# A layer of attention and routed experts: rows and activations of the routed stage turned by VectorE and ScalarE instead of TensorE

## The reference

```python
x = x + cross_attention(layernorm(x), ctx_1024)        # 1024 tokens of 512, 1601 keys each of 16 batches
x = x + relative_attention(layernorm(x), ...)
x = x + ffn(layernorm(x), ...)                         # ffn is a block of its own:
#   x = x + mla(rmsnorm(x, w_ln1), ...)
#   x = x + moe(rmsnorm(x, w_ln2), ...)
def moe(xn, ...):                                      # xt: 1024 tokens x 512
    shared = silu(xt @ Wg_s) * (xt @ Wu_s) @ Wd_s
    probs = sigmoid(xt @ W_router + routing_bias)      # 7 experts
    scores, idx = top_k(probs, 2)
    scores = scores / sum(scores)
    for each of the two experts e of a token:          # Wg_r, Wu_r, Wd_r are 7 x 512 x 512
        out += score * ((silu(xt @ Wg_r[e]) * (xt @ Wu_r[e])) @ Wd_r[e])
    return shared + out
```

## Time and profile before

| | us |
|---|---|
| median of 3 runs | 813.64 |
| lowest and highest | 810.62, 814.64 |
| profiled execution, whole | 809.95 |
| profiled execution, its span | 808.1 |
| mean granted TensorE clock | 0.994 of full speed |

### The profile page before, as it was taken

The page is one execution under the profiler, slowest core; times in us unless marked ns, Lnnn a source line. Parts: engine busy times, 40 slices in busy tenths (PEclk is TensorE's granted clock), DMA queues, the critical chain, the costliest instruction groups (busy, mean ns, idle before and its releaser), DMA issues.

```text
span 808.1 us, 17427 instructions
## 1 busy us (share of the span) xinstructions
PE 773.6 (96%) x6752; PEld 574.0 (71%) x6753; DVE 517.4 (64%) x1125; ACT 355.5 (44%) x913; POOL 301.0 (37%) x157
## 2 busy tenths in 40 slices
PE   4799999999899999989999999899999999999996
PEld 3555455554657778878867877788888888888884
DVE  5799798788652447777788887855364333443335
ACT  4356545661443248852178768523432122211221
POOL 1000000000442833732032213533649999993034
PEclk9999999999899999999999999999999999999999
DMA  9968756683520050040388000030485355531138
GB/s 341 390 252 327 259 218 243 262 326 122 219 105 1 0 149 13 2 138 0 105 312 314 1 0 1 22 137 25 183 306 210 112 206 167 191 135 52 52 114 275
DMA packets 46576, 127.04 MB, mean 157 GB/s; under 512 B 4001, under 2 KB 8353, under 8 KB 40369
## 3 DMA queue, kind: packets, MB, share of 16 engines
q1 hardware_dynamic: 36752, 105.44, 35.9%
q10 hardware_dynamic: 7200, 12.32, 4.4%
q0 software_dynamic: 2560, 8.39, 3.1%
HBM read 101.99 MB, written 24.15 MB: 156 GB/s over the span
## 4 chain that ended last, share of the span: by engine, by line
PE 81%; DVE 5%; DMA 5%; POOL 3%; ACT 3%; issue 2%; SPq 0%; DVEq 0%; ACTq 0%; POOLq 0%
PE scores L611 11%; PE bank L641 11%; PE bank L1137 7%; PE bank L1139 7%; PE bank L1138 7%; DMA nat<-in_ctx_keys 3%; PE bank L691 2%; POOL picked L1379 2%; PE bank L845 2%; PE bank L693 2%; PE bank L851 2%; PE bank L692 2%; PE bank L846 2%; PE bank L626 2%; PE bank L881 2%
## 5 line engine op out<-in xcount | busy, mean ns | idle before, releaser
L1844 DVE STREAM_TRANSPOSE ctxT<-nat 128x1024 f32<-128x1024 f32 (+3 forms) x124 | 116.9, 1004 | 7.8 <-DMA nat<-in_ctx_keys 7.5
L641 PE MATMUL bank<-nat,probT 128*64 128x512 f32 (+1 forms) x416 | 93.9, 597 | 0.1
L1366 POOL TENSOR_TENSOR ring_lo<-ring_raw,ring_hi 128x2048 fp32r<-128x2048 f32 x18 | 83.0, 4611 | 14.5 <-ACT ring_hi L1732 13.3
L1244 POOL TENSOR_TENSOR wq_lo<-wq_raw,wq_hi 128x1024 fp32r<-128x1024 f32 x4 | 9.3, 2352 | 207.6 <-ACT wq_hi L1477 207.6
L1137 PE MATMUL bank<-ring_hi,xg_lo 128*128 x180 | 74.2, 412 | 0.0
L1139 PE MATMUL bank<-ring_hi,xg_hi 128*128 x180 | 70.6, 392 | 0.0
L1138 PE MATMUL bank<-ring_lo,xg_hi 128*128 x180 | 70.1, 389 | 0.0
L2488 DVE TENSOR_TENSOR rhm_lo<-bank,rhm_hi 128x512 fp32r<-128x512 f32 x21 | 14.5, 692 | 80.2 <-ACT rhm_hi L1743 80.2
L641 PEld LDWEIGHTS bank<-nat,probT 128*64 128x64 f32 (+1 forms) x416 | 27.9, 136 | 51.6 <-issue 48.1
L1749 ACT COPY hn<-bank 128x512 f32<-128x512 f32 x22 | 12.9, 588 | 112.0 <-PE bank L1139 112.0
L611 PE MATMUL scores<-ctxT,hn 32*64 32x416 f32 (+8 forms) x1536 | 55.2, 426 | 5.1 <-issue 2.7
(11 more groups left out here) (317 smaller groups left out, 1936.1 us busy)
## 6 DMA issues: line engine op xcount, KB each, us to landing
nat<-in_ctx_keys SPq DMA_DIRECT2D x48, 1024.0 KB, 8.1
ring_raw<-in_Wexp SPq DMA_DIRECT2D x21, 1024.0 KB, 6.3
x_slots<-zeros SPq DMA_DIRECT2D x1, 5632.0 KB, 18.2
y_slots<-zeros SPq DMA_DIRECT2D x1, 5632.0 KB, 32.7
hn<-x_slots ACTq DMA_DIRECT2D x22, 256.0 KB, 4.5
y_slots<-hn ACTq DMA_DIRECT2D x22, 256.0 KB, 3.0
w_raw<-in_Wexp SPq DMA_DIRECT2D x3, 1024.0 KB, 5.3
nat<-in_ctx_keys SPq DMA_DIRECT2D x16, 130.0 KB
```

The lines of the kernel that those rows point to most:

```text
L641: last = nc.tensor.matmul(context_bank(k)[64 * b:64 * b + 64, :], probT[0:n, j, 64 * b:64 * b + 64], nat[k % 2][0:n, b, j, :], start=j == ...
L1366: last = nc.gpsimd.tensor_tensor(ring_lo[at], ring_raw[at], ring_hi.bitcast(F32)[at], ALU.subtract)
L1844: dve.transpose(dst, src).then_inc(columns_ready, 1)
```

## The change

Four things are changed.

1. **Rows.** `xg` is loaded by four DMAs of 32 partitions each instead of one of 128. Each moves 128 pieces of 512 bytes (`slot_rows`), and they are issued three tiles ahead. DVE turns the tile in blocks of 32 x 32 straight into PSUM (`xgT`, banks 6 and 7). The order of the features that comes out is made good by weights that are permuted before the launch (`by_block`). The low part's last quarter waits for the expert's weights (`rows_end`).
2. **Activations.** After its multiplication DVE turns `rhm` in 32 x 32 blocks into `rhm_blocks`. ACT moves these by 16 copies of 32 partitions x 128 elements to their places in bank 3. DVE makes both the high and the low part. The last tile keeps PE's transposes. On DVE the rows of tile t+2 are prepared between the multiplication and the split of tile t. On ACT the 16 copies of tile t come before the output of tile t-1.
3. **Entrance.** The second expert's down matrix is loaded as soon as the shared expert's products are done, and the other two when the first two tiles' rows have landed. POOL and ACT take the down matrix first (`order_of`, `second_high(2)`). DVE prepares the rows of tile 0 before it adds the output of block 6 and before the low part of the first expert's down matrix.
4. **Router.** Each of its matmuls becomes four of 32 columns of weights.

```diff
-        xg = hn[0:2]
+        xg = [t.rearrange("p (g f) -> p g f", f=P) for t in hn[0:2]]
+        xgT = [b[:].rearrange("p (a q) -> p a q", q=P) for b in bank[6:8]]
+        rhm_blocks = place(156, "rhm_blocks", [P, HC, 4, B32])
+        rhmT = bank[3][:].rearrange("p (c q) -> p c q", q=P)
+        def slot_rows(t):
+            return x_slots[ds(t * P, P), :].rearrange("(g q) (c f) -> c q g f", q=B32, f=P)
+        def order_of(e):
+            return (2, 0, 1) if e == 1 else (0, 1, 2)
...
                     sp.wait_ge(gu_full, NJ)
-                    sp.wait_ge(scattered, 16 * 2 * NT)
-                for m in range(3):
+                for m in order_of(e):
+                    if e == 1 and m == 0:
+                        for landed in xg_loaded:
+                            sp.wait_ge(landed, 64)
...
                 for c in range(HC):
-                    last = nc.tensor.matmul(bank[3][:, NE * k:NE * k + NR], xf[k % 4][:, c, :], wrout_sb[:, c, :],
-                                            start=c == 0, stop=c == HC - 1)
+                    for m in range(P // B32):
+                        own = slice(B32 * m, B32 * (m + 1))
+                        last = nc.tensor.matmul(bank[3][own, NE * k:NE * k + NR], xf[k % 4][:, c, own], wrout_sb[:, c, :],
+                                                start=c == 0, stop=c == HC - 1, skip_group_check=True)
...
             def load_rows(t, par):
-                nc.scalar.dma_start(xg[par][:], x_slots[ds(t * P, P), :]).then_inc(xg_loaded[par], 16)
+                for c in range(HC):
+                    nc.scalar.dma_start(xg[par][B32 * c:B32 * (c + 1)], slot_rows(t)[c]).then_inc(xg_loaded[par], 16)
             def hidden_columns_out(t):
-                act.wait_ge(rhmT_full, t + 1)
-                nc.scalar.copy(hidden_parts(t)[0][:].rearrange("p c q -> p (c q)"), bank[3][:]).then_inc(rhm_split, 1)
+                act.wait_ge(rhm_turned, 2 * t + 1)
+                if isinstance(t, int) and t == TILES - 1:
+                    last = nc.scalar.copy(rhm_last[0][:].rearrange("p c q -> p (c q)"), bank[3][:])
+                else:
+                    for g in range(4):
+                        for a in range(4):
+                            last = nc.scalar.copy(rhmT[B32 * a:B32 * (a + 1), :, B32 * g:B32 * (g + 1)],
+                                                  rhm_blocks[B32 * g:B32 * (g + 1), :, a, :])
+                last.then_inc(rhm_split, 1)
+            act.wait_ge(slots_ready, 5)
+            second_high(2)
             act.wait_ge(scattered, 16 * 2 * NT)
...
             def routed_step(t, par, turn, load=True):
                 if load:
-                    act.wait_ge(xgT_full, t + 1)
-                    load_rows(t + 2, par)
+                    act.wait_ge(xgT_full, t + 2)
+                    load_rows(t + 3, 1 - par)
                 routed_silu(t)
-                if isinstance(t, int) and t == TILES - 1:
-                    hidden_columns_out(t)
-                    output_rows(t - 1, 1 - par, turn)
-                else:
-                    output_rows(t - 1, 1 - par, turn)
-                    hidden_columns_out(t)
+                hidden_columns_out(t)
+                output_rows(t - 1, 1 - par, turn)
...
+            def rows_columns(t, par, turn):
+                dve.wait_ge(xg_loaded[par], 64 * turn)
+                dve.transpose(xgT[par].rearrange("p a (g q) -> p a g q", q=B32),
+                              xg[par].rearrange("p g (a e) -> p a g e", e=B32)).then_inc(xgT_full, 1)
...
             def routed_mult(t):
                 dve.tensor_tensor(rhm[:], rhm[:], bank[2][:], ALU.mult).then_inc(rhm_ready, 1)
+                if not (isinstance(t, int) and t == TILES - 1):
+                    dve.wait_ge(rhm_ready, t + 1)
+                    dve.transpose(rhm_blocks[:].rearrange("p c a q -> p (c a q)"), rhm[:]).then_inc(rhm_turned, 1)
             def hidden_split(t):
+                dve.tensor_copy(rhm_hi[:], rhmT).then_inc(rhm_turned, 1)
+                dve.wait_ge(rhm_turned, 2 * t + 2)
+                dve.tensor_tensor(rhm_lo[:], rhmT, rhm_hi.bitcast(F32)[:], ALU.subtract).then_inc(rhmT_ready, 1)
...
+            def hidden_and_next(t, par, turn):
+                nth = need_of(t + 2)
+                routed_mult(t)
+                rows_columns(t + 2, par, turn + 1)
+                hidden_split(t)
+                rows_end(par, nth)
```

More of the change, by code:

```diff
@@ L1140, in routed_product, with routed_hidden @@
                 last.then_inc(full, 1)
-            def rows_columns(t, par, turn):
-                pe.wait_ge(xg_loaded[par], 16 * turn)
-                if not (isinstance(t, int) and t < 2):
-                    pe.wait_ge(xgT_ready, t - 1)
-                for c in range(HC):
-                    last = nc.tensor.transpose(bank[6 + par][:, c * P:(c + 1) * P], xg[par][:, c * P:(c + 1) * P], ident)
-                last.then_inc(xgT_full, 1)
-            def routed_hidden(t, par, at, turn=None):
-                if not (isinstance(t, int) and t < 2):
-                    hidden_columns(t - 1)
+            def routed_hidden(t, par, at):
                 pe.wait_ge(xgT_ready, t + 1)
@@ L1223, in _ @@
             routed_hidden(TILES - 1, 1, at[1])
-            hidden_columns(TILES - 1)
+            last_hidden_columns()
             routed_output(TILES - 2, 0, at[0])
@@ L1359, in _ @@
             for e in range(1, NR):
-                for m in range(3):
+                for n, m in enumerate(order_of(e)):
                     pool.wait_ge(routed_loaded[m], 16 * (e + 1))
@@ L2452, in down_out @@
                 dve.tensor_tensor(y[:, k, :], bank[k % 4][:], y[:, k, :], ALU.add).then_inc(down_added, 1)
-            for k in range(NT - 1):
-                down_out(k)
-                if 3 <= k < 6:
-                    m = k - 3
-                    dve.wait_ge(split_hi, m + 1)
-                    at = (slice(None), PLACES[0], m)
-                    last = dve.tensor_tensor(ring_lo[at], ring_raw[at], ring_hi.bitcast(F32)[at], ALU.subtract)
-                    if m == 2:
-                        last.then_inc(split_ready, 1)
@@ L2467, in rows_columns_out @@
                 dve.wait_ge(xgT_full, t + 1)
-                columns = [bank[6 + par][:, c * P:(c + 1) * P] for c in range(HC)]
-                weights = [vec[:, V_W2 + c:V_W2 + c + 1] for c in range(HC)]
                 for c in range(HC):
-                    last = dve.tensor_scalar(xg_hi[par][:, c, :], columns[c], weights[c], None, ALU.mult)
+                    last = dve.tensor_scalar(xg_hi[par][:, c, :], xgT[par][:, c, :], vec[:, V_W2B + c:V_W2B + c + 1], None, ALU.mult)
                 last.then_inc(xg_split, 1)
@@ L2473, in rows_columns_out, with rows_low @@
                 dve.wait_ge(xg_split, t + 1)
-                dve.wait_ge(split_ready, nth)
-                for c in range(HC):
-                    last = dve.scalar_tensor_tensor(xg_lo[par][:, c, :], columns[c], weights[c], xg_hi[par].bitcast(F32)[:, c, :],
-                                                    ALU.mult, ALU.subtract)
-                last.then_inc(xgT_ready, 1)
+                for c in range(HC - 1):
+                    rows_low(par, c)
+            def rows_low(par, c):
+                return dve.scalar_tensor_tensor(xg_lo[par][:, c, :], xgT[par][:, c, :], vec[:, V_W2B + c:V_W2B + c + 1],
+                                                xg_hi[par].bitcast(F32)[:, c, :], ALU.mult, ALU.subtract)
@@ L2480, in routed_mult, with rows_end @@
+            def rows_end(par, nth=None):
+                if nth is not None:
+                    dve.wait_ge(split_ready, nth)
+                rows_low(par, HC - 1).then_inc(xgT_ready, 1)
             def routed_mult(t):
@@ L2491, in _ @@
-            rows_columns_out(0, 0)
-            down_out(NT - 1)
-            rows_columns_out(1, 1)
-            routed_mult(0)
-            hidden_split(0)
-            with dve.Fori(0, TILES // 2 - 1) as i:
+                if isinstance(t, int) and t == TILES - 1:
+                    hi, lo = rhm_last
+                    dve.tensor_tensor(lo[:].rearrange("p c q -> p (c q)"), bank[3][:],
+                                      hi.bitcast(F32)[:].rearrange("p c q -> p (c q)"), ALU.subtract).then_inc(rhmT_ready, 1)
+                    return
@@ new lines, in hidden_split @@
+                if not (isinstance(t, int) and t == 0):
+                    dve.wait_ge(rdown_full, t)
+                dve.tensor_copy(rhm_hi[:], rhmT).then_inc(rhm_turned, 1)
+                dve.wait_ge(rhm_turned, 2 * t + 2)
+                dve.tensor_tensor(rhm_lo[:], rhmT, rhm_hi.bitcast(F32)[:], ALU.subtract).then_inc(rhmT_ready, 1)
+            for k in range(NT - 2):
+                down_out(k)
+                if k in (3, 4):
+                    first_low(k - 3)
+            rows_columns(0, 0, 1)
@@ new lines, in _ @@
+            rows_end(0)
+            down_out(NT - 2)
+            first_low(2).then_inc(split_ready, 1)
```

(7 more changed lines are left out.)

65 lines of the change are left out of this document (30 added, 35 removed).

## The result

| | us |
|---|---|
| changed kernel, median of 4 runs (lowest, highest) | 827.18 (825.61, 829.73) |
| kernel before, median of 4 runs | 814.14 |
| ratio | 1.017, 95% interval 1.014 to 1.020 |
| profiled execution of the changed kernel, its span | 829.73, 827.9 |

The change makes the kernel slower by 1.7%. The forecast was 833 us, with 811 to 847 as its range.

The account below looks back on a forecast made before the run. ACT's loop with DVE was to bound the routed stage: entrance +5.0, 17 longer periods +17.7, step 19 -2.0, end +1.0, together +21.7 on 809.95, plus 1.8 for the median, gives 833 us. Range 811 to 847.

Parts of the forecast that it names:

- ACT's loop with DVE: Routed stage: silu, DVE's work, 16 copies, output copy, store and four loads run in sequence, above PE's 8.23 us.
- The signs it named: Routed stage: ACT's longest waits not for PE, PE waiting 1.9 us a tile before the down product, POOL with gaps.
- The period: Routed stage, from one tile's silu to the next: 10.15 us, against 9.11 before.
- Copies: ACT's 16 copies of 32 x 128 in a tile, without overlap: 0.31 us each, 4.9 us together.
- Store and loads: End of ACT's step: store issue 0.36, four load issues 2.0, and 0.04 us to the next silu.
- Silu to first copy: Start of ACT's step: silu, DVE's multiplication and turning, with hand-overs, 2.07 us.
- The rule that spoke against it: Trainium skill: back-to-back activations overlap by about 93 ns; the copies would lie 200 ns apart, 3.2 us for 16.
- The sum: Whole kernel: entrance, 17 longer periods, a step without loads and the end together add 21.7 us.
- to the silu of tile 2: Entrance: silu of tile 2 at about 619.5 instead of 614.48, +5.0 us, the router's gain lost behind ACT's queue.
- Rival 1: Routed stage: copies overlap, the loop is 8.5 us and POOL holds tile 16; 804 us (806 median), chance 0.12.
- Rival 3: Routed stage: PE's clock falls in its new gaps, 850 to 860 us, or issues are worse, 847; chance 0.08.
- Rival 2: ACT's loop: copies at 0.26 and loads at 1.5 give 8.85 us, 807 to 811, no change; chance 0.08.

Follow-up runs that it names:

- experiment 1: Changed kernel, with ACT issuing each routed step's four row loads behind the silu instead of ahead of it; 811.11 us, ratio to the kernel before 0.9989.
- 7: Changed kernel, with each tile's rows fetched by one DMA of 128 rows in place of four of 32, computing something else; 810.86 us, ratio 0.9974.
- 6: Changed kernel, with eight more ACT copies of 32 x 128 per tile into a tile that nothing reads; 874.35 us, ratio 1.0756.
- experiment 8: Changed kernel, with the 16 copies written to the partitions they are read from, computing something else; 812.1 us in one run.
- experiment 10: Changed kernel, with the 16 copies made in place over 128 partitions x 32 elements instead of 32 x 128; 806.86 us in one run.
- experiment 5: experiment 1, with DVE's wait for an expert's split weights cut in two, gate and up parts first, down part later; 808.92 us, ratio 0.9959.
- 9: experiment 5, with both of a step's register reads moved to the step's head, in front of the multiplication; 807.36 us, ratio 0.9935.
- 11: Kernel 9, with both register reads moved between the next tile's split and DVE's wait for the copies; 802.27 us, ratio 0.9896.
- experiment 3: Kernel before, with only the router's products made 32 columns wide; 809.26 us, ratio 0.9976.

## Why the prediction was right

**The mechanism.** The prediction said that ACT's loop with DVE takes the bound from PE, with nothing in it overlapping. Experiments 1 and 7 show it, and 6 agrees: moving the loads out of the loop, taking issues from it and adding copies to it change the period by what the part lasts, until the next bound. The signs it named are there: the silu waits for its own queue, PE waits before the down product (20.1 us in 16 waits, the longest 2.3), POOL has gaps (17.06 busy of 20). The wait was forecast as 1.9 us a tile and is 1.3. The loop is 0.14 us shorter, and the profile counts less than PE has to spare: it lets a wait begin at the end of the last matmul, 0.39 us after its start, where matmuls in a row start 0.23 us apart.

**Its terms.** The period was to be 10.15 us (the terms as written add up to 10.14) and is 10.01 ((781.22 - 621.01) / 16).
- Copies: 4.9 forecast, 4.35 measured. The kind was right (no overlap, 12 ns between copies, as in the earlier trace rows); the length was too high, 297 ns for 261. The row is a copy from SBUF to SBUF. Experiment 6 has both side by side: its extra copies into SBUF last 297 ns, just the number worked out, those into PSUM 261. The two groups of that kernel, from 600 to 780 us:

```profile
L1743 ACT COPY bank<-rhm_blocks 32x128 f32<-32x128 f32 x238 | 62.0, 261 | 25.0 <-DVE rhm_blocks L2496 22.4
L1746 ACT COPY spare<-rhm_blocks 32x128 f32<-32x128 f32 x120 | 35.6, 297 | 1.2
```

- Store and loads: 2.40 forecast (0.36 + 2.0 + 0.04), 2.84 or 2.42 measured in turn, up to 3.75 in the few long steps, 2.78 on average over the 16 periods. The four issues last 1.8 as the earlier trace rows suggested, but stand 0.2 to 0.6 us behind the store's. These 0.38 us make up for most of the copies' error of 0.6, and only so does the period come out within 0.14 us: the sizes of both terms were off.
- Silu to first copy: 2.07 forecast, 2.17 measured.

**The rule that spoke against it.** The Trainium skill (ScalarE: Activation LUTs, What ACT_TABLE_LOAD costs) gives an overlap of some 93 ns between activations in a row. The traces decide: none for the 16 copies of the changed kernel (261 long, 273 apart), 54 to 60 ns for copies in place within one group of 32 partitions (experiment 8), 60 over all 128 (experiment 10: 180, 120). The rule's length for 128 elements, 186 + 128 x 0.833, gives an estimate of 293 ns; the copy into SBUF agrees with it (297), the one into PSUM doesn't (261).

**The sum.** Between the two profiled executions lie 19.8 us, where the sum had 21.7. It is not made of the terms as I had them. The transposes that feed the router start 5.1 us later than in the kernel before, ahead of all that the change touches, as the first starts of L984 in before and of L997 in after show:

```profile
L984 PE MATMUL bank<-cst,xx x16: 272/273/328, 513.0 to 517.5; 128*128 128x128 f32 x16
```

```profile
518.09 1.04 PE L997 MATMUL bank<-cst,xx 128*128 128x128 f32 x8
```

This is for the most part variation between executions. Kernels 1, 5, 9 and 11 have the same program as the changed one up to these transposes, which start in them at 515.39, 518.32, 513.42 and 513.69, and the first silu at 600.45, 603.20, 598.59 and 598.99 (603.24 in the changed one). The profiled execution of before (809.95) was faster than all of its four timed runs, that of after the slowest of its four. So it is in part luck that 19.8 lies so near 21.7. The rest is:

| part | forecast | measured |
|---|---|---|
| ahead of the change | 0 | +5.1 |
| to the silu of tile 2 | +5.0 | +1.4 |
| tiles 2 to 19, 17 steps (one without loads) | +15.7 | +12.8 (167.7 - 154.9) |
| silu of 19 to the output copy of 18, and on | +1.0 | +0.5 |

So the change itself costs 14.7 us in these two executions and 13.0 by the medians, and the forecast was some 7 us too high: 3 in the steps (the copies), 3.6 in the entrance. There the router gave its gain (2 us in experiment 3, 2.7 forecast), and the second expert's other two matrices landed as forecast (601.4 and 604.5, less the 5.1 us 596.3 and 599.4; forecast 596 and 599.5). A part of the error are the copies of tiles 0 and 1, counted with 4.9 us too: those of tile 0 ended at 605.6 (less the 5.1 us, as all times here; forecast 606.3). But the larger part is that I had let ACT's issues follow its copies, and there they run beside them. Three issues ahead of the silu of tile 1 were to hold it until 608.2, and it started at 606.2; the four ahead of the silu of tile 2 were to cost 2.0 us behind the four small multiplications, and lay beside them. Together that is some 2.5 of the 3.6 us. The silu of tile 2 started at 615.9 (forecast 619.5). In the trace of the changed kernel, at the end of tile 0's copies:

```profile
609.33 0.32 ACTq L1729 DMA_DIRECT2D hn<-x_slots  x1
609.59 0.26 ACT L1742 COPY bank<-rhm_blocks 32x128 f32<-32x128 f32 x1
609.68 0.45 ACTq L1729 DMA_DIRECT2D hn<-x_slots  x1
609.86 0.53 ACT L1742 COPY bank<-rhm_blocks 32x128 f32<-32x128 f32 x2
610.16 0.45 ACTq L1729 DMA_DIRECT2D hn<-x_slots  x1
```

In a step of the stage the issues can't do this, since the store, which waits for the output copy, stands ahead of them.

**The rivals.** Rival 1, POOL at tile 16, was wrong for this kernel, since its condition (copies that overlap) failed. But its second half is what experiment 1 ran into when the loop was shortened in another way: it put the silu of tile 16 at 740.7 and the time at 804 to 806; experiment 1 has 743.41 and 811. Rival 3: the clock stayed at full speed from tile 2 to the end of the stage, as forecast. It fell at the entrance (0.79 from 611 to 615 us, 0.82 from 615 to 620), where PE waited 2.3 us, and time and again in experiment 6. Rival 2's issues and copies were half right (copies of 0.26, issues not cheap).

**What stays open.** Experiment 11 gains 11.9 us against before from tile 2 to tile 19 and 7.8 over the span. Of the rest 1.8 lie ahead of tile 2 and 2.3 behind the silu of tile 19. Of these 1.4 lie between that silu and the output copy of tile 18 (7.42 us against 5.98), where the 16 copies of tile 19 now stand; for the other 0.8, behind that copy, I have no cause. Why the loads start 0.58 us late in every second step was not tried; the loop's branch stands there. And the two executions of the kernels with the old order (before and experiment 3: 513.0 and 513.8 at the router's transposes) are too few to say that none of the 5.1 us comes from the change.

## What to carry to other kernels

When work is taken off a full engine and given to idle ones, add up the loop that the receiving engine's program order makes, DMA issues and hand-overs included: 53% busy can be the bound. Then move what nobody waits for (here four issues and two register reads) into that engine's waits. And look at who was second before: in experiment 1 POOL took back in one wait the 6.6 us that the tiles had gained on the kernel before, until the wait was cut to the part that is needed first.

## What was not expected of the hardware

- A copy of 32 x 128 by ACT takes 261 ns into PSUM and 297 into SBUF.
- ACT's copies of 32 partitions in a row overlap by 54 to 60 ns when each writes to the same group of 32 as the last write into that memory, and stand 12 ns apart when the group changes, even where the copy stays on its own partitions (experiments 6 and 8, the changed kernel; read from the traces).
- ACT's DMA issues run beside its own copies where nothing ahead of them waits (609.33 to 610.61 in the changed kernel); in the stage they stand behind a store that does.
- On DVE a register read from SBUF takes part of a microsecond of its stream: between copy and split lie 0.85 us with one read (experiment 5) and 0.12 without.
